# A decoder layer on one core: norm roots as powers on GpSimd, exponentials spaced by TensorE's time, x reloaded in pieces, the any-key applied once

## The reference, cut to what matters

```python
def _layernorm(x): return (x - mean(x)) / sqrt(var(x) + 1e-5)

def attn(x):                                     # selective scan, 16 states
    xp = x @ x_proj_w.T;  dt_in, B, C = split(xp, [16, 32])
    dt = softplus(dt_in @ dt_proj_w.T + dt_proj_b)
    h_t = exp(dt_t * A) * h_(t-1) + dt_t * B_t * x_t;   y_t = sum_n h_t * C_t
    return y + D * x

def xattn(h, ctx, m):                            # 32 heads of 128
    z = rmsnorm(h) * ln_weight
    q, k, v = z @ w_q.T, ctx @ w_k.T, ctx @ w_v.T
    score = where(m, q @ k.T + position_bias, -inf)
    return h + (where(m, softmax(score), 0) @ v) @ w_out.T

def ffn(x): return x @ W.T + b + einsum('bser,e,eor', x @ A.T, probs, B)

x = x + attn(_layernorm(x), ...)
x = x + xattn(_layernorm(x), ctx_4096, mask, ...)
x = x + ffn(_layernorm(x), ...)
```

## Time and profile before

| | |
|---|---|
| median of three runs | 967.6 us (966.61 to 967.91) |
| the profiled execution | 968.25 us |
| its span | 966.3 us |
| TensorE busy | 929.5 us (96%) |
| VectorE busy | 613.1 us (63%) |
| ScalarE busy | 516.3 us (53%) |
| GpSimd busy | 505.6 us (52%) |
| mean granted clock | 0.989 |

### The profile page before, as it was taken

The page is one execution under the profiler, slowest core; times in us unless marked ns, Lnnn a source line. Parts: engine busy times, 40 slices in busy tenths (PEclk is TensorE's granted clock), DMA queues, the critical chain, the costliest instruction groups (busy, mean ns, idle before and its releaser), DMA issues.

```text
span 966.3 us, 14589 instructions
## 1 busy us (share of the span) xinstructions
PE 929.5 (96%) x4648; PEld 764.9 (79%) x4648; DVE 613.1 (63%) x711; ACT 516.3 (53%) x1174; POOL 505.6 (52%) x266
## 2 busy tenths in 40 slices
PE   8989989999999999798999999999999999999998
PEld 6666667788878878687888888888888888888776
DVE  5589878789989999245444444444544444444675
ACT  4776756666665664345455444454454555544631
POOL 3135688897757676424444444444544444444422
PEclk9999999999999999899999999999999999999999
DMA  8444576566566654154444444446444444444302
GB/s 290 160 132 142 157 249 184 171 189 197 194 196 195 196 153 174 44 183 139 139 142 147 139 138 147 149 151 226 149 142 138 139 144 146 138 142 147 113 2 87
DMA packets 96720, 150.03 MB, mean 155 GB/s; under 512 B 10464, under 2 KB 35168, under 8 KB 96560
## 3 DMA queue, kind: packets, MB, share of 16 engines
q1 hardware_dynamic: 87888, 132.72, 42.1%
q10 hardware_dynamic: 8800, 16.91, 7.2%
HBM read 113.81 MB, written 35.78 MB: 155 GB/s over the span
## 4 chain that ended last, share of the span: by engine, by line
PE 51%; issue 17%; DVE 12%; POOL 10%; ACT 5%; DMA 3%; POOLq 0%; SPq 0%; ACTq 0%; DVEq 0%
PE acc L425 11%; PE acc L427 10%; PE acc L426 10%; DVE misc L1078 4%; POOL wo_lo L1332 4%; POOL bm L1328 4%; PE misc L426 3%; PE misc L427 3%; PE misc L425 3%; PE acc L635 3%; PE acc L660 3%; DVE w L1085 2%; DVE misc L1073 2%; PE acc L625 2%; DMA k_scratch<-kst 2%
## 5 line engine op out<-in xcount | busy, mean ns | idle before, releaser
L1312 POOL TENSOR_TENSOR wq_lo<-wq_raw,wq_hi 128x512 fp32r<-128x512 f32 x64 | 85.1, 1329 | 278.4 <-ACT wq_hi L874 278.4
L1280 POOL TENSOR_TENSOR y<-y,w 128x2048 f32<-128x2048 f32 x32 | 147.6, 4611 | 75.0 <-DVE w L1085 74.5
L1172 DVE TENSOR_TENSOR ot_lo<-acc,ot_hi 128x512 fp32r<-128x512 f32 x64 | 44.3, 692 | 174.8 <-ACT ot_hi L939 174.8
L1078 DVE TENSOR_TENSOR_SCAN misc<-dA,misc 128x2048 f32<-128x2048 f32 x32 | 141.7, 4429 | 15.5 <-ACT dA L744 12.9
L932 ACT ACTIVATE prob<-prob,negm 128x128 f32<-128x128 f32 x256 | 99.8, 391 | 80.2 <-DVE negm L1156 80.2
L425 PE MATMUL acc<-wv_hi,ctx_hi 128*128 128x512 f32 x256 | 103.1, 403 | 8.9 <-ACT vst L728 8.2
L921 ACT ACTIVATE q_sb<-acc 128x512 f32<-128x512 f32 x64 | 38.3, 598 | 134.8 <-PE acc L427 134.8
L425 PE MATMUL acc<-z_hi,wq_hi 128*128 128x512 f32 x256 | 106.2, 415 | 0.3 <-POOL wq_lo L1312 0.3
L425 PE MATMUL misc<-wo_hi,ot_hi 128*128 128x512 f32 x256 | 106.5, 416 | 0.0
L425 PE MATMUL acc<-ctx_hi,wk_hi 128*128 128x512 f32 x240 | 95.9, 400 | 7.4 <-ACT kst L722 6.7
L426 PE MATMUL misc<-wo_lo,ot_hi 128*128 128x512 f32 x256 | 101.7, 397 | 0.0
(11 more groups left out here) (160 smaller groups left out, 1947.9 us busy)
## 6 DMA issues: line engine op xcount, KB each, us to landing
k_scratch<-kst SPq DMA_DIRECT2D x64, 256.0 KB, 2.7
bc<-xp_scratch ACTq DMA_DIRECT2D x32, 512.0 KB, 5.2
v_scratch<-vst SPq DMA_DIRECT2D x32, 512.0 KB, 3.6
wq_raw<-in_wq SPq DMA_DIRECT2D x64, 256.0 KB, 3.3
k_sb<-k_scratch SPq DMA_DIRECT2D x64, 256.0 KB, 2.5
v_sb<-v_scratch SPq DMA_DIRECT2D x64, 256.0 KB, 2.6
wo_raw<-in_wo SPq DMA_DIRECT2D x64, 256.0 KB, 2.9
wraw<-in_wk SPq DMA_DIRECT2D x32, 256.0 KB, 4.6
```

Source lines behind the costliest of these rows:

```text
L1078: dve.tensor_tensor_scan(h_ps, flat(dA[k % 2][:, :, :, :]), h_ps, 0.0, ALU.mult, ALU.add).then_inc(da_free, 1)
L1172: dve.tensor_tensor(ot_lo[p][:], psO, ot_hi[p][:].bitcast(F32), ALU.subtract).then_inc(ot_lo_done, 1)
L1280: pool.tensor_tensor(y_half(half), y_half(half), w[:, k % 2], ALU.add).then_inc(y_ready, 1)
L1312: pool.tensor_tensor(wq_lo[p][:], wq_raw[p][:], wq_hi[p][:].bitcast(F32), ALU.subtract).then_inc(wq_lo_done, 1)
```

## The change

1. `inverse_root` moves to GpSimd: `(v + eps) ** -0.5` with `ALU.pow`. ScalarE's logarithm and exponential and VectorE's refinement go. For the middle norm GpSimd also makes the factors of `new_base` (`mix`); ScalarE applies them for half 0.
2. `due` spaces exponentials by the time of the slots passed (`T_SUM`, `T_EXP`, in units of 10 ns); `EARLY` is 11. `b_copy` is at the first exponential of a step. The norm's hooks are at steps 24 and 26.
3. The first softplus runs in two parts, its two last additions in another order; the second one's exponential and logarithm are tied to slots (`EXP_AT`, `LOG_AT`) and cut in two. A one-element exponential stands behind the first logarithm.
4. `x` is reloaded into `base` by eight DMAs, each behind a K store of groups 5 and 6, in place of one in front of group 2.
5. The last addition into `y` is made by VectorE in four parts, `low_z` is two steps earlier, and the z transposes stand before Q of head 0. One V sum is moved to step 2.
6. In the heads, VectorE's reciprocal and product follow the exponentials in the same step; `anykey` is a factor in `add_sums`.
7. `WARM` is 40; the first sums take `wk_lo` before `ctx_lo`; `f_input(1)` stands before the fourth FFN product.

```diff
-WARM = 24
+WARM = 40
 ENTRY = 4
 KZ = 12
 Y_AT = KP
-ROOT_AT = KP + 3
-EARLY = 13
+EARLY = 11
...
+HOOKS = (24, 26)
+T_SUM, T_TR, T_XP, T_DT, T_EXP = 273, 45, 340, 85, 234
 
 
 def due(s):
 
-    sums = s - XT[0] - sum(s > t for t in XT + [XP] + DT + YT + ZT)
-    return min(C * NSTEP, EARLY + 8 * (sums + (s > XP) + (s > DT[-1])) // 7)
+    single = {**{t: T_TR for t in XT + YT + ZT}, **{t: T_DT for t in DT}, XP: T_XP}
+    e = EARLY + sum(single.get(t, T_SUM) for t in range(XT[0] + 1, s)) // T_EXP
+    return min(C * NSTEP, e - sum(e > C * k for k in HOOKS))
+EXP_AT = DT[-1] + 2
+LOG_AT = next(s for s in range(slot(1, 0), slot(NG, 0)) if due(s) >= 11 * C - 2)
...
+            def load_x(b):
+                sp.dma_start(base[:, b], a["x"][b]).then_inc(x_again[b // HB], 16)
+            def k_group(g, at=5, x_half=None):
                 for j in range(KP):
                     k_store(g, j)
+                    if x_half is not None and j < HB:
+                        load_x(x_half * HB + j)
...
-            sp.wait_ge(sum_evac, DT[-1] + 1)
-            sp.wait_ge(xp_stored, 32)
-            sp.dma_start(base[:], a["x"].rearrange("b t d -> t b d")).then_inc(x_again, 16)
...
+                k_group(g, x_half=g - 5)
...
-                pe.wait_ge(ctx_lo_done, c + 1)
                 pe.wait_ge(wk_lo_0, c + 1)
                 for j in range(4):
                     w_part, m_part = slice(j // 2 * P, (j // 2 + 1) * P), slice(j % 2 * HT, (j % 2 + 1) * HT)
-                    pe.matmul(acc[:, j], wk_hi[:, c, w_part], ctx_lo[:, c, m_part], start=False, stop=False)
-                    mm = pe.matmul(acc[:, j], wk_lo[:, c, w_part], ctx_hi[:, c, m_part], start=False, stop=(c == C - 1))
+                    pe.matmul(acc[:, j], wk_lo[:, c, w_part], ctx_hi[:, c, m_part], start=False, stop=False)
+                pe.wait_ge(ctx_lo_done, c + 1)
+                for j in range(4):
+                    w_part, m_part = slice(j // 2 * P, (j // 2 + 1) * P), slice(j % 2 * HT, (j % 2 + 1) * HT)
+                    mm = pe.matmul(acc[:, j], wk_hi[:, c, w_part], ctx_lo[:, c, m_part], start=False, stop=(c == C - 1))
...
-            pe.wait_ge(y_ready, NSTEP)
             for b in range(HB):
+                pe.wait_ge(y_ready, NSTEP + b)
                 y_transpose(HB + b, misc[:, b]).then_inc(yt_ps, 1)
             v_group(NG - 1, range(KZ - KP))
+            pe.wait_ge(yt_evac, HB)
+            for c in range(C):
+                z_transpose(1, c, misc[:, c]).then_inc(zt_ps, 1)
...
-                    pe.wait_ge(yt_evac, HB)
-                    for c in range(C):
-                        z_transpose(1, c, misc[:, c]).then_inc(zt_ps, 1)
                 if g == 1:
-                    for b in range(KZ - KP + 2, B):
-                        v_sum(NG - 1, b)
+                    v_sum(NG - 1, B - 2)
+                if g == 2:
+                    pe.wait_ge(pt_evac, 1)
+                    v_sum(NG - 1, B - 1)
...
-                if half:
-                    f_input(1, *((x2_done, HB + c + 1) for c in range(C)))
                 for b in range(half * HB, (half + 1) * HB):
                     if half:
                         pe.wait_ge(out_ready, b - HB + 1)
+                    if b == HB - 1:
+                        f_input(1, *((x2_done, HB + c + 1) for c in range(C)))
...
-            def inverse_root(n, kinds, bs):
-                act.wait_ge(ln_var, n)
-                act.activation(tmp8[:, kinds, bs], var[:, kinds, bs], ACT.Ln).then_inc(ln_log, 1)
-                act.wait_ge(ln_log, n)
-                act.activation(rstd[:, kinds, bs], tmp8[:, kinds, bs], ACT.Exp, scale=-0.5).then_inc(ln_exp, 1)
...
-                        if k == 6:
-                            softplus_1("exp")
-                        if k == 10:
-                            softplus_1("log")
                         if k == 15:
-                            y0_copy(1)
-                        if k == 25:
-                            inverse_root(3, both, of_half(0))
...
-            act.activation(anykey[:, 0:1], ident[:, 0:1], ACT.Ln, bias=1.0)
+            act.activation(anykey[:, 0:1], ident[:, 0:1], ACT.Exp)
...
+            for part in range(2):
+                cs = slice(2 * part, 2 * part + 2)
+                for c in range(2 * part, 2 * part + 2):
+                    act.wait_ge(sp_max, c + 1)
+                    act.activation(w[:, 0, c], misc[:, c], ACT.Abs, bias=dtb[:, c:c + 1]).then_inc(sp_abs, 1)
+                act.wait_ge(sp_abs, 2 * part + 2)
+                act.activation(w[:, 0, cs], w[:, 0, cs], ACT.Exp, scale=-1.0).then_inc(sp_exp, 1)
             k_copy(0, 7)
-            act.wait_ge(sp_exp, 1)
+            act.wait_ge(sp_exp, 2)
             act.activation(u[:, 0], w[:, 0], ACT.Ln, bias=1.0).then_inc(sp_log, 1)
-            split_w(2, wk_hi)
             v_copy(0, 0)
             v_copy(0, 1)
+            act.activation(mix[:, 0, 0:1], negA[:, 0, 0:1], ACT.Exp)
...
             emitted = exps(0, C)
+            v_copy(0, 2)
+            split_w(2, wk_hi)
             v_copy(0, 3)
-            y0_copy(0)
+            y0_copy(0, range(2))
+            v_copy(0, 4)
+            y0_copy(0, range(2, C))
             emitted = exps(emitted, C + 2)
...
+            def new_base_0(b):
+                act.wait_ge(zn_done, b + 1)
+                act.wait_ge(mix_ready, 1)
+                act.activation(base[:, b], base[:, b], ACT.Identity, scale=mix[:, 1, b:b + 1], bias=mix[:, 0, b:b + 1]).then_inc(base_mixed, 1)
...
+                    s = slot(g, j)
+                    if s != LOG_AT + 1:
+                        emitted = exps(emitted, due(s))
+                    if EXP_AT <= s <= EXP_AT + 1:
+                        softplus_1("exp", s - EXP_AT)
+                    if LOG_AT <= s <= LOG_AT + 1:
+                        softplus_1("log", s - LOG_AT)
...
+            for part in range(2):
+                e, r = flat(w[:, 0, 2 * part:2 * part + 2]), rest_f[:, part * 2 * HT:(part + 1) * 2 * HT]
+                dve.wait_ge(sp_exp, part + 1)
+                link(dve.tensor_scalar(r, e, 1.0, -1.0, ALU.add, ALU.add))
+                dve.tensor_tensor(r, e, r, ALU.subtract).then_inc(sp_rest, 1)
+            dve.wait_ge(sp_rest, 2)
+            dve.wait_ge(sp_max, C)
+            link(dve.tensor_tensor(flat(dt_[:, 0]), flat(dt_[:, 0]), rest_f, ALU.add))
             dve.wait_ge(sp_log, 1)
-            link(dve.tensor_tensor(rest_f, rest_f, flat(u[:, 0]), ALU.add))
-            dve.wait_ge(sp_max, C)
-            dve.tensor_tensor(flat(dt_[:, 0]), flat(dt_[:, 0]), rest_f, ALU.add).then_inc(sp_done, 1)
+            dve.tensor_tensor(flat(dt_[:, 0]), flat(dt_[:, 0]), flat(u[:, 0]), ALU.add).then_inc(sp_done, 1)
...
-            def refine(n, kinds, bs):
-                dve.wait_ge(ln_exp, n)
-                v, r, t = var[:, kinds, bs], rstd[:, kinds, bs], tmp8[:, kinds, bs]
-                link(dve.tensor_tensor(t, r, r, ALU.mult))
-                link(dve.tensor_tensor(t, t, v, ALU.mult))
-                link(dve.tensor_scalar(t, t, -0.5, 1.5, ALU.mult, ALU.add))
-                link(dve.tensor_tensor(r, r, t, ALU.mult))
...
+            dve.wait_ge(prod_done, NSTEP)
+            for b in range(HB):
+                dve.tensor_tensor(y[:, HB + b], y[:, HB + b], w[:, (NSTEP - 1) % 2, :, b], ALU.add).then_inc(y_ready, 1)
...
-                    dve.wait_ge(exp_done, g - 1)
-                    dve.reciprocal(rec[p][:], psum[p][:]).then_inc(rec_done, 1)
-                    dve.wait_ge(rec_done, g - 1)
-                    dve.tensor_tensor(rec[p][:], rec[p][:], anykey[:, sh * HB:(sh + 1) * HB], ALU.mult).then_inc(recv_done, 1)
-                    dve.wait_ge(recv_done, g - 1)
-                    dve.tensor_tensor(prob[p][:], prob[p][:], rec[p][:, :].unsqueeze(2).to_broadcast([P, HB, S]),
-                                      ALU.mult).then_inc(p_ready, 1)
...
+                if runs(g - 1):
+                    dve.wait_ge(exp_done, g)
+                    dve.reciprocal(rec[q][:], psum[q][:]).then_inc(rec_done, 1)
+                    dve.wait_ge(rec_done, g)
+                    dve.tensor_tensor(prob[q][:], prob[q][:], rec[q][:, :].unsqueeze(2).to_broadcast([P, HB, S]),
+                                      ALU.mult).then_inc(p_ready, 1)
...
+                    i = half * HB + b
+                    dve.scalar_tensor_tensor(base[:, i], misc[:, b], anykey[:, i:i + 1], base[:, i], ALU.mult,
+                                             ALU.add).then_inc(x2_done, 1)
...
+            def inverse_root(n, half, both=False):
+                bs = slice(half * HB, (half + 1) * HB)
+                kinds = slice(0, 2) if both else 0
+                pool.wait_ge(ln_stats, n)
+                if both:
+                    pool.tensor_scalar(var[:, 1, bs], mv[:, bs, 1], 1.0 + EPS, EPS * EPS, ALU.mult, ALU.add)
+                pool.tensor_scalar(var[:, 0, bs], mv[:, bs, 1], 1.0, EPS, ALU.mult, ALU.add).then_inc(ln_var, 1)
```

(30 more changed lines are left out.)

131 lines of the change are left out of this document (55 added, 76 removed).

## The result

The changed kernel takes 937.27 us (median of 4 runs, 935.63 to 938.61), the kernel before 967.41 (966.61 to 967.91) beside it: a ratio of 0.9687, 95% interval 0.9675 to 0.9698, so 3.1% faster. The forecast was 938.4. The executions of one kernel lie within 0.3% here and up to 0.7% in the experiments, wider than the 0.15% told at the start. The profiled execution took 937.41 us, its span is 935.6, and 30.7 us are gone from the span.

The account below looks back on a forecast made before the run. It took TensorE's queue plus its pauses as the bound. Gains of 6.3 + 9.2 + 8.9 + 5.6 + 0.2 less 1.0 made 29.2 us off the profiled 968.25: 939.0, or 938.4 as median; range 932 to 950.

Parts of the forecast that it names:

- first term: From the start to the first transposes of the second half: TensorE gets there 6.3 us earlier, at 64.8 us.
- The warm-up step: Kernel start: `WARM` 40 for 24 costs 1.6 us, lower clock (1.7) and short waits (0.7) go: 0.8 net gain.
- The softplus step: First half's softplus: `dt_` ends at 40.2, the logarithm starts near 44.0, the first scan at 53.5, 7.4 us earlier.
- From there to the wait for `y`: Second-half transposes to the `y` wait: 8.0 us of waits plus 3.2 of clock, less 2 given back: 9.2 us.
- The reload's part: Copy at 143.38 us: 4.0 us of TensorE wait, plus 1.6 of clock, go when `x` reloads in eight pieces.
- The wait for `y`: TensorE's wait for the last addition into `y` goes: 8.9 us, 6.5 of wait and 2.4 of clock.
- Heads: Head stage: five waits for VectorE's `prob`, 5.9 us, go except 0.3: 5.6 us gained.
- the charge for the power: Roots on GpSimd, showing before the last transposes and at the z chain: 1.0 us taken off the gain.
- the rival of scalar code at p = 10: GpSimd's power takes 10 us for four elements, open at five of six roots: 983 us; slow powers overall 5%.
- The scan as bound: ScalarE's delays stay, VectorE's scan ends at 375.4 and TensorE waits about 4 us for `y`: 943 us, 15%.
- The moved pauses: Pauses only move, to the K stores between reload pieces, the z chain, heads and softplus: 949 us, 15%.
- The planner without effect: New spacing of exponentials does nothing; scan level and TensorE's K-sum waits as before: 955 us, 3%.

Follow-up runs that it names:

- the old rule at 11: Changed kernel with the exponentials spaced by the previous counting rule (8/7 for each sum) and `EARLY = 11`: 943.82 us, ratio 0.9765 to the kernel before.

## Why the prediction was right in its sum and wrong in its first term

**To the first transposes of half two: 6.3 us forecast, 2.6 measured.** This is the term that was mis-sized. Two steps failed: the gain of the warm-up, and the chain of the softplus, which took for granted that the low clock was gone.

The warm-up step said 0.8 net. I priced the 16 further matmuls at 0.224 us each, 1.6 in all; all 40 took 6.12 us and the first real matmul still stands at 8.98, beside 8.87. They cost nothing, and the first transposes of x came 2.1 us earlier, at 23.02 instead of 25.15. But I looked only at TensorE. ScalarE's x copies were bound by the K stores and stood still at 27.8, so all 2.1 us became the wait at L505: nothing net. The projection matmul stands at 30.01, where it stood at 29.98 before.

The softplus step said that the first scan would start at 53.5. VectorE and ScalarE after:
```profile
41.43 0.75 DVE L1045 TENSOR_SCALAR dt_<-misc,dtb 128x512 f32<-128x512 f32 x1 [0.95 <-PE misc L510]
...
57.51 4.43 DVE L1085 TENSOR_TENSOR_SCAN misc<-dA,misc 128x2048 f32<-128x2048 f32 x1
```
```profile
46.45 0.60 ACT L732 ACTIVATE kst<-acc 128x512 f32<-128x512 f32 x1 [2.46 <-PE acc L440]
47.07 1.28 ACT L834 ACT_TABLE_LOAD   x1
48.36 1.92 ACT L834 ACTIVATE u<-w 128x2048 f32<-128x2048 f32 x1
...
52.48 1.28 ACT L837 ACT_TABLE_LOAD   x1
```
The last `dt_` piece ends at 42.2, not 40.2, since TensorE made it at the low clock; and the logarithm waits behind a K copy that waits for TensorE, at 48.36 rather than 44.0. The scan starts 3.4 us earlier, not 7.4. With the clock up, as in the run with the logarithm in one piece, `dt_` ends at 40.8, the logarithm starts at 45.0, the first scan at 54.6 and the transposes at 65.1, where the forecast had 40.2, 44.0, 53.5 and 64.8. So the softplus chain was right to about 1 us for an execution whose clock stays up. I had let the low windows of the earlier trace rows go and allowed none in their place. Instead 3.4 us of low clock came at 35 to 50 us. It is not shown that the new wait at the projection brings it: the clock fell there also behind a wait of 0.3 us or none. Its cause stays open.

**From there to the wait for `y`: 9.2 forecast, 11.2 measured.** The sum had 11.2 before I gave 2 back; that step was too careful. But its parts were not as forecast. The waits of this stretch fell from 12.4 to 5.1 us, 7.3 and not 8.0; both low windows went, 3.4; 0.5 is left that I can't assign. The reload's part was too small: put back, it costs 7 to 8 us, not 5.6. For the logarithm I had credited the halving, and in one piece it costs TensorE nothing. What differs from before are the V copy between the logarithm and the second load and the weight split behind, which were not tried apart. The planner, which I had called a possible loss (2.34 us each against 9.35 a step), is needed to keep both the copies and the scan on time.

The scan is where I was further off: its last `w` ends at 370.9, not at 360, though inside the bounds 353 to 375.4. It starts 4.0 us later than forecast. Of the 22.4 us of waits I took 15.4 as given back, and 11.0 were: the waits for the copy of B (11.5) are gone, those for the exponentials hardly shrank:
```profile
DVE misc L1085 <- ACT dA L754: 11.4, 7, 3.1
```
The other 2.5 us of the miss I can't assign. So the scan is nearly the bound: the last additions run from 371.02 to 373.5, and TensorE comes at 374.75, 1.2 us behind.

**The wait for `y`: 8.9 forecast.** Held: no wait. The last addition on GpSimd brought 5.0 us of it back. z after the change, as VectorE's timeline has it:
```profile
371.02 2.50 DVE L1127 TENSOR_TENSOR y<-y,w 128x512 f32<-128x512 f32 x4
...
385.19 1.92 DVE L1016 TENSOR_SCALAR y<-base,mv,rstd 128x512 f32<-128x512 f32 x4 [2.31 <-POOL rstd L1255]
```
VectorE waits 2.31 us for the root, where it waited 6.42; I had allowed about 2, and the z transposes at 387.44 have no pause.

**Heads: 5.6, and 0.2 for `f_input(1)`.** Held: both waits are gone, with 0.3 more than forecast. Behind the `y` wait the sum said 8.9 + 5.6 + 0.2 - 1.0 = 13.7 and the trace has 16.9. Of the 3.2 more, 1.0 is the charge for the power, which reached TensorE nowhere; 0.3 is the `prob` rest; about 0.6 is a head step of 7.773 instead of 7.783 us (means of six and seven steps from 500 us on), sixty times; some 1.3 I can't assign.

**The power: 1.0 us taken.** The row says 1.03 for four elements, 1.65 for eight, so the guess of a size was right and the rival of scalar code at p = 10 is excluded. The charge on TensorE was too high by all of it. One reading in that rival was wrong: the 2.29 us set against GpSimd's addition is VectorE's product with C, not an addition.

**The table loads.** The trace after sides with the earlier trace rows: 1.28 us at 47.07 ahead of the logarithm and again at 52.48 between it and the next exponential. The section "Table sets: the hidden batching unit" of the Trainium skill's "ScalarE: Activation LUTs" would have the second one missing; in this kernel it isn't. In the kernel before each root had two loads, the very first one a single one, and none of these is left.

**Rivals.** The scan as bound (943): not as built, but it shows with 1.6 us in the old rule at 11. The moved pauses (949): no; `kst` waits shrank. The planner without effect (955, for which the prediction shows no working): no, it has 6 to 7 us. Slow powers: no. The sum came out 1.1 us off the median because 3.7 too much in the first term stood against 2.0 and 3.2 too little in the others. That they cancelled was luck; so was part of the 3.7, since with the clock up the first term is 6.0.

## What to carry to other kernels

An earlier start of one engine is worth only what the in-order queue of the next lets through: look for the instruction that stands at the same time before and after, and what it waits for (here three copies behind stores). A pause costs its length; the lower clock behind it is a separate term. Here it came behind a wait and without one, and stayed away in other executions, so allow some 3 us between executions for it and compare times at the same mean clock. Before you cut an instruction in two, look at the whole row of work between two copies. A share "given back" that no row shows is better kept in the range than in the sum.
